# Attention between batches in the last encoder: two tiles of four heads a step

## The chip, the cores and the metric

The kernel runs on one NeuronCore of one Trainium2 chip. Its engines are TensorE (PE, with its weight loads PEld), VectorE (DVE), ScalarE (ACT), GpSimd (POOL) and SyncE (SP), each with a queue of its own. The metric is the device time of one execution in microseconds; lower is better.

## The reference

Four layers follow each other on x of 8 batches, 256 tokens and 128 channels. The last one's encoder holds the attention of this case. It attends between batches: its sequence is the batch index, and each of the 256 token places is a problem of its own with 8 queries and 8 keys.

```python
def _mha(x, w, b, ow, ob):          # L = 8 batches, N = 256 places, H = 4 heads, HD = 32
    L, N, _ = x.shape
    qkv = x @ w.T + b
    q, k, v = jnp.split(qkv, 3, axis=-1)
    rh = lambda t: t.reshape(L, N, H, HD).transpose(1, 2, 0, 3)
    q, k, v = (rh(q), rh(k), rh(v))
    scores = jnp.einsum('nhld,nhmd->nhlm', q, k) / np.float32(np.sqrt(HD))
    attn = jax.nn.softmax(scores, axis=-1)
    o = jnp.einsum('nhlm,nhmd->nhld', attn, v).transpose(2, 0, 1, 3).reshape(L, N, D)
    return o @ ow.T + ob
```

Around it stand layer norms and a mixture of eight experts, which the change does not touch.

## The kernel before

The kernel is a chain of stages, each of several programs (nc.Block); all engines meet at the end of a program. encoder3 (L2730) calls batch_attention (L2960) first.

The 2048 tokens are laid in 16 tiles of 128: a tile holds 16 token places of all 8 batches. The scores of a tile are 128x128 per head; a mask table, same_token, is 0 where two columns belong to the same place and -1e30 elsewhere, so that the softmax runs over the 8 batches of one place.

After a layer norm and the transposing of the weights there are three programs:
- Queries, keys and values (L2993 to L3034): PE makes queries and keys by channels (L3000) into the four banks of psS, DVE copies them with bias and in tile order (L3018), ACT permutes x (L3028), PE makes the values by tokens (L3008), and DVE adds their bias (L3022). A bank is overwritten once DVE has copied it.
- Attention (class SmallAttention, L2743): 64 units, each of one tile and one head, written as two loops over the 16 tiles, one loop for two heads. For a unit DVE masks the queries to the rows of one head (L2856), PE makes the scores over all 128 rows (L2827), DVE adds the mask and takes the maximum (L2872) and negates it (L2884), ACT takes the exponential with a running sum (L2919), PE transposes (L2835), DVE and ACT in turn copy the result (L2910), PE multiplies by the head's 32 value columns (L2847), and DVE takes the reciprocal (L2895) and scales the product into att_out (L2897). PE's order interleaves the scores of the next unit with the transpose and the product of this one. Exponentials, copies and transposes are each of one unit.
- Projection (L3057 to L3093): PE transposes the 16 tiles of att_out (L3066), ACT copies them back to token order (L3082), PE multiplies by the output weights (L3071), DVE has added the bias to XN meanwhile (L3088) and adds the product (L3092).

Of the kernel before, what the change touches and what calls it, by code (L numbers as in the profile page):

```python
# [52 lines left out]
def constants():  # L53
# [37 lines left out]
    tables["swap"] = swap  # L91
    place, at = {}, 0
# [2650 lines left out]
class SmallAttention:  # L2743
# [3 lines left out]

    masked_queries = True

    def __init__(self, k, mem, chunks, groups, hd, heads, masks=False, like=None):
        self.k, self.chunks, self.groups, self.hd, self.heads, self.masks = k, chunks, groups, hd, heads, masks
        self.NC, self.G = len(chunks), len(groups)
        width = chunks[-1][0] + chunks[-1][1]
        if like is not None:
            self.q = like.q
            self.prob = like.prob  # L2760
            self.probT = like.probT
            self.masked = like.masked
            self.peak = like.peak
            self.shift = like.shift
            self.sums = like.sums
            self.total = like.total
            self.rtotal = like.rtotal
            self.waiter = like.waiter
        else:
            self.q = k.sb("att_q", [P, 2, P], ctx=mem)  # L2770
            self.prob = k.sb("att_prob", [P, 2, width], ctx=mem)
            self.probT = k.sb("att_probT", [P, self.G, BANK], ctx=mem)
            self.masked = k.sb("att_masked", [P, width], ctx=mem) if masks else None
            self.peak = k.sb("att_peak", [P, 2, self.NC], ctx=mem)
            self.shift = k.sb("att_shift", [P, 2], ctx=mem)
            self.sums = k.sb("att_sums", [P, 2, self.NC], ctx=mem)
            self.total = k.sb("att_total", [P, 2], ctx=mem)
            self.rtotal = k.sb("att_rtotal", [P, 2], ctx=mem)
            self.waiter = k.sb("att_waiter", [P, 2, self.NC], ctx=mem)
        self.q_ready, self.score_ready = k.flag("q_ready"), k.flag("score_ready")  # L2780
        self.peak_done, self.shift_ready = k.flag("peak_done"), k.flag("shift_ready")
        self.exp_done, self.turned = k.flag("exp_done"), k.flag("turned")
        self.values_done, self.total_done = k.flag("values_done"), k.flag("total_done")
        self.rtotal_done, self.out_free = k.flag("rtotal_done"), k.flag("out_free")
        self.slot = [k.psO[:, 0, 0:hd], k.psM[:, 0:hd]]
        self.copied = [k.flag("copied_by_dve"), k.flag("copied_by_act")]

    def finish(self, blocks):

        units = blocks * self.heads * 2  # L2790
        self.q_ready.passed(units if self.masked_queries else 0)
        self.score_ready.passed(units * self.NC)
        self.peak_done.passed(units * self.NC)
        self.shift_ready.passed(units)
        self.exp_done.passed(units * self.NC)
        self.turned.passed(units * self.G)
        self.values_done.passed(units)
        self.total_done.passed(units if self.NC > 1 else 0)
        self.rtotal_done.passed(units)
        self.out_free.passed(units + 2)  # L2800
        self.copied[0].passed(units * self.G // 2 + 1)
        self.copied[1].passed(units * self.G // 2 + 1)

    def credit(self, eng, engine):

        if engine == "dve":
            eng.sem_inc(self.out_free.sem, 2)
            eng.sem_inc(self.copied[0].sem, 1)  # L2810
        else:
            eng.sem_inc(self.copied[1].sem, 1)

    def pe_step(self, pe, keys_of, values_of, score=None, value=None):

        k, nc, NC, G = self.k, self.k.nc, self.NC, self.G
        for c in range(max(NC, G) + 2):
            if value is not None and c < max(NC, G):
                j, s, h = value

                pe.wait_ge(*self.exp_done((j * 2 + s) * NC + c + 1))
            if score is not None and c < NC:
                js, ss, hs = score
                if c == 0:
                    pe.wait_ge(*self.q_ready(js * 2 + ss + 1))
                c0, w = self.chunks[c]
                nc.tensor.matmul(k.psS[:, c, 0:w], self.q[:, ss, :], keys_of(hs, ss, c0, w),  # L2827
                                 start=True, stop=True).then_inc(self.score_ready.sem, 1)
            if value is not None and c < G:
                n = s * G + c  # L2830

                pe.wait_ge(*self.copied[n % 2](j * G + n // 2 + 1))
                at = 0
                for b, (col, w) in enumerate(self.groups[c]):
                    last = nc.tensor.transpose(k.psT[0:w, n % 2, b * P:(b + 1) * P],  # L2835
                                               self.prob[:, s, col:col + w], k.ident)
                last.then_inc(self.turned.sem, 1)
            g = c - 2
            if value is not None and 0 <= g < G:
                n = s * G + g  # L2840
                if g == 0:

                    pe.wait_ge(*self.out_free(j * 2 + s + 1))

                pe.wait_ge(*self.copied[n % 2](j * G + n // 2 + 2))
                for b, (col, w) in enumerate(self.groups[g]):
                    last = nc.tensor.matmul(self.slot[s], self.probT[0:w, g, b * P:(b + 1) * P],  # L2847
                                            values_of(h, s, g, b, w),
                                            start=(g == 0 and b == 0), stop=(g == G - 1 and b == len(self.groups[g]) - 1))
                if g == G - 1:  # L2850
                    last.then_inc(self.values_done.sem, 1)

    def dve_queries(self, dve, q_of, s, h):

        src, head_column = q_of(h, s)
        self.k.nc.vector.tensor_scalar(self.q[:, s, :], src, head_column, None, ALU.mult).then_inc(self.q_ready.sem, 1)  # L2856

    def dve_step(self, dve, out_of, mask_of, score=None, value=None):
        k, nc, NC, G = self.k, self.k.nc, self.NC, self.G
        for c in range(max(NC, G)):  # L2860
            if score is not None and c < NC:
                j, s, h = score
                c0, w = self.chunks[c]
                if not self.masks:
                    dve.wait_ge(*self.score_ready((j * 2 + s) * NC + c + 1))
                    nc.vector.tensor_reduce(self.peak[:, s, c:c + 1], k.psS[:, c, 0:w], AX_X,
                                            ALU.max).then_inc(self.peak_done.sem, 1)
                else:

                    dve.wait_ge(*self.score_ready((j * 2 + s) * NC + c + 1))  # L2870
                    nc.vector.memset(self.waiter[:, s, c:c + 1], 0.0)
                    nc.vector.tensor_tensor_reduce(out=self.masked[:, c0:c0 + w], in0=k.psS[:, c, 0:w],  # L2872
                                                   in1=mask_of(s, c0, w), scale=1.0, scalar=NEG_BIG, op0=ALU.add,
                                                   op1=ALU.max, accum_out=self.peak[:, s, c:c + 1]).then_inc(self.peak_done.sem, 1)
            if value is not None and c < G:
                jv, sv = value[0], value[1]
                n = sv * G + c
                if n % 2 == 0:
                    dve.wait_ge(*self.turned((jv * 2 + sv) * G + c + 1))
                    self.copy(nc.vector.tensor_copy, c, 0, self.copied[0])  # L2880
        if score is not None:

            dve.wait_ge(*self.peak_done((j * 2 + s) * NC + NC))
            nc.vector.tensor_reduce(self.shift[:, s:s + 1], self.peak[:, s, :], AX_X, ALU.max,  # L2884
                                    negate=True).then_inc(self.shift_ready.sem, 1)
        if value is not None and len(value) == 3:
            jv, sv, hv = value

            dve.wait_ge(*self.values_done(jv * 2 + sv + 1))
            total = self.sums[:, sv, 0:1]  # L2890
            if NC > 1:
                total = self.total[:, sv:sv + 1]
# [7 lines left out]
    def copy(self, how, g, bank, signal):  # L2900
# [3 lines left out]
        for b, (col, w) in enumerate(group):  # L2904
            if runs and runs[-1][2] == w:
                runs[-1][1] = b + 1
            else:
                runs.append([b, b + 1, w])
# [405 lines left out]
```

## Time and profile before

| | us |
|---|---|
| median of 3 runs | 5033.36 (5023.75 to 5037.87) |
| profiled execution, first to last instruction | 5038.9 |
| PE busy in it | 4122.8 (82%) |
| DVE busy | 3247.9 (64%) |
| ACT busy | 2417.4 (48%) |
| POOL busy | 1405.9 (28%) |
| mean granted clock of PE | 0.865 |

The span runs from the first to the last instruction of the profiled execution; the page gives no other time of that execution, so its span stands for it. Busy shares are means over stages that have different limits: what counts for this change is the stretch from 4682 to 4870 us. In the rows below, x48 is a count of records, and an fp32 matmul is two records (a transpose is one). "128*64 128x256" is a weight tile of 128 rows and 64 columns and a moving operand of 256 columns. The granted clock has two levels, 1.2 and 2.4 GHz; 0.50 means that the lower one was granted throughout, and a matmul's own duration shows which it ran at.

### The profile page before, as it was taken

The page shows a single profiled execution, that of the slowest core. Times are in us where ns is not written, and L with a number is a line of the kernel's source. Part 1 is how long each engine was busy: PE and PEld are TensorE (multiplying, and loading weights), DVE is VectorE, ACT ScalarE, POOL GpSimd, SP SyncE. Part 2 cuts the span into 40 slices and gives each one's busy share as a digit, 9 for nine tenths or more (in the row PEclk, how much of TensorE's full clock was granted, in tenths as well). Part 3 has the DMA queues.
Part 4 walks back from the last instruction along what each step waited for, and adds up shares of the span by engine and source line. Part 5 has one row for each costly group of instructions (what it writes and reads, how often), then busy time and mean ns, then how long its engine had stood idle before and what let it go on. Part 6 is the DMA issues. An engine that isn't in the chain of part 4 may idle for free. (4 is left out here: it accounts for less than half of the span.)

```text
span 5038.9 us, 78227 instructions
## 1 busy us (share of the span) xinstructions
PE 4122.8 (82%) x28631; PEld 2518.8 (50%) x28631; DVE 3247.9 (64%) x5963; ACT 2417.4 (48%) x4632; POOL 1405.9 (28%) x1137
## 2 busy tenths in 40 slices
PE   3499999589299965688877899999999999998554
PEld 2133333378033323466664566666666666665342
DVE  3499999422377647433333687888787778887546
ACT  2288888233199840233331455555555554554320
POOL 0200000000300000111100466566566566665000
PEclk6599999699599975677778999999999999999557
DMA  5222221000354200000000000000000000000001
GB/s 155 63 53 46 42 54 33 1 24 14 59 82 75 41 3 17 7 0 0 0 7 27 26 14 1 14 1 14 1 14 14 1 14 1 1 1 1 5 9 38
DMA packets 119688, 122.83 MB, mean 24 GB/s; under 512 B 21264, under 2 KB 97648, under 8 KB 118992
## 3 DMA queue, kind: packets, MB, share of 16 engines
q1 hardware_dynamic: 119240, 118.20, 11.0%
q8 instruction: 197, 3.23, 0.3%
q14 instruction: 107, 0.88, 0.1%
q10 hardware_dynamic: 144, 0.52, 0.0%
HBM read 102.94 MB, written 15.73 MB: 24 GB/s over the span
## 5 line engine op out<-in xcount | busy, mean ns | idle before, releaser
L831 DVE TENSOR_REDUCE att_peak.1<-psS 128x1 f32<-128x512 f32 (+1 forms) x1024 | 580.4, 631 | 94.2 <-PE psS L701 94.1
L2633 POOL TENSOR_TENSOR key_sums_0.1<-key_sums_0.1,prob_0.1 128x512 f32<-128x512 f32 x256 | 402.4, 1572 | 29.0 <-POOL key_sums_0.1 L2628 0.4
L800 ACT ACTIVATE att_probT.1<-psT 128x512 f32<-128x512 f32 (+1 forms) x682 | 368.7, 568 | 75.7 <-PE psT L730 34.3
L2633 POOL TENSOR_TENSOR key_sums_1.1<-key_sums_1.1,prob_1.1 128x512 f32<-128x512 f32 x256 | 386.1, 1508 | 28.7 <-POOL key_sums_1.1 L2633 0.4
L831 DVE TENSOR_REDUCE att_peak.2<-psS 128x1 f32<-128x512 f32 (+1 forms) x512 | 266.8, 568 | 145.0 <-PE psS L701 143.2
L2472 ACT COPY prob_0.1<-psS 128x1024 f32<-128x1024 f32 (+1 forms) x224 | 203.7, 954 | 323.3 <-PE psS L2371 323.3
L701 PE MATMUL psS<-key_stack.1,query_stack.1 64*128 64x512 bf16 (+1 forms) x1024 | 271.1, 386 | 94.1 <-DMA key_stack.1<-key_parts 47.3
L2472 ACT COPY prob_1.1<-psS 128x1024 f32<-128x1024 f32 (+1 forms) x224 | 203.7, 954 | 296.3 <-PE psS L2371 296.3
L747 PE MATMUL psM<-att_probT.1,quad_values.1 128*9 128x256 f32 (+1 forms) x3840 | 306.0, 391 | 19.4 <-issue 19.4
L2542 DVE TENSOR_TENSOR att_highest.1<-att_highest.1,prob_1.1 128x1024 f32<-128x1024 f32 (+1 forms) x160 | 280.4, 1753 | 53.7 <-ACT prob_1.1 L2472 46.4
L2542 DVE TENSOR_TENSOR att_highest.1<-att_highest.1,prob_0.1 128x1024 f32<-128x1024 f32 (+1 forms) x160 | 270.8, 1692 | 56.5 <-ACT prob_0.1 L2472 49.9
L1934 POOL TENSOR_TENSOR head_queries.1<-queryT.1,query_sin.1 64x256 f32<-64x256 f32 x128 | 92.2, 720 | 699.3 <-DVE queryT.1 L2002 691.8
L2628 POOL TENSOR_TENSOR key_sums_0.1<-prob_0.1 128x512 f32<-128x512 f32 x64 | 95.8, 1496 | 587.9 <-ACT prob_0.1 L2478 587.9
L701 PEld LDWEIGHTS psS<-key_stack.1,query_stack.1 64*128 64x128 bf16 x1024 | 78.2, 93 | 352.8 <-issue 192.3
L2563 DVE TENSOR_TENSOR prob_0.1<-prob_0.1,psO 128x1024 f32<-128x1024 f32 (+1 forms) x256 | 245.8, 1011 | 0.0
L2563 DVE TENSOR_TENSOR prob_1.1<-prob_1.1,psO 128x1024 f32<-128x1024 f32 (+1 forms) x256 | 245.7, 1010 | 0.0
L803 ACT ACTIVATE att_probT.2<-psT,att_key_bias.1 128x256 f32<-128x256 f32 (+1 forms) x554 | 224.0, 480 | 27.6 <-PE psT L730 23.8
L2351 PE MATMUL psT<-wkv.1,ctxT_0.1 128*128 128x128 f32 (+1 forms) x1664 | 214.3, 280 | 12.9 <-DVE ctxT_1.1 L2521 12.9
L2351 PE MATMUL psT<-wkv.1,ctxT_1.1 128*128 128x128 f32 (+1 forms) x1664 | 214.6, 280 | 10.9 <-DVE ctxT_0.1 L2521 9.7
L701 PE MATMUL psS<-key_stack.2,query_stack.2 102*128 102x512 bf16 (+1 forms) x512 | 144.5, 367 | 94.7 <-DMA key_stack.2<-mask_parts 87.8
L2341 PE MATMUL psM<-ctxT_0.1,wkv.1 128*128 128x512 f32 (+1 forms) x512 | 215.5, 544 | 3.3 <-ACT keyT_0.1 L2455 1.9
L2351 PEld LDWEIGHTS psT<-wkv.1,ctxT_0.1 128*128 128x128 f32 (+1 forms) x1664 | 192.2, 187 | 50.7 <-issue 31.4
(675 smaller groups left out, 9298.7 us busy)
## 6 DMA issues: line engine op xcount, KB each, us to landing
key_stack.1<-key_parts SPq DMA_DIRECT2D x384, 58.0 KB
key_stack.2<-key_parts SPq DMA_DIRECT2D x96, 200.1 KB
ctx_rows.1<-in_ctx_dram SPq DMA_DIRECT2D x8, 1536.0 KB
key_parts<-split_parts.1 SPq DMA_DIRECT2D x8, 1200.8 KB, 5.7
ctx_keys_0.1<-in_ctx_dram SPq DMA_DIRECT2D x4, 768.0 KB
ctx_keys_1.1<-in_ctx_dram SPq DMA_DIRECT2D x4, 768.0 KB
query_stack.1<-query_parts SPq DMA_DIRECT2D x192, 16.0 KB
ctx_values_0.1<-in_ctx_dram SPq DMA_DIRECT2D x4, 768.0 KB
```

The lines of the kernel that those rows point to most:

```text
L701: self.k.nc.tensor.matmul(self.score_bank[m % 3][:, 0:w], self.queries(rows, g, h, s * P, P), self.keys(rows, g, h, c0, w), start=True, st ...
L747: last = self.k.nc.tensor.matmul(self.partial[32 * j:32 * j + self.hd + 1, :], self.vquad[0:w, q % 2, blk, j, :], self.probT[0:w, g % self ...
L800: last = self.k.nc.scalar.activation(probs[:, blks[0]:blks[-1] + 1, :].rearrange("p b q -> p (b q)"), bank[0:w, 0:len(blks) * S], ACT.Exp)
L803: last = self.k.nc.scalar.activation(probs[:, blk, :], bank[0:w, n * S:(n + 1) * S], ACT.Exp, bias=bias)
L831: self.k.nc.vector.tensor_reduce(self.peak[:, 2 * h + s, c:c + 1], self.score_bank[m % 3][:, 0:w], AX_X, ALU.max).then_inc(self.peak_done. ...
L2341: last = nc.tensor.matmul(bank[:, 0:w], self.wkv[:, t, p * P:(p + 1) * P], self.ctxT[b % 2][:, t, n * BANK:n * BANK + w], start=(t == 0), ...
L2351: last = nc.tensor.matmul(bank[0:w, kb % 4 * P:(kb % 4 + 1) * P], self.ctxT[b % 2][:, t, kb * P:kb * P + w], self.wkv[:, t, at:at + P], st ...
L2472: nc.scalar.copy(self.prob[i % 2][:, :, at:at + w], k.psS[:, 2 * (g % 2):2 * (g % 2) + 2, 0:w]).then_inc(self.kept.sem, 1)
L2542: self.k.nc.vector.tensor_tensor(own, old, new, ALU.max).then_inc(self.raised.sem, 1)
L2563: self.k.nc.vector.tensor_tensor(own, own, by, ALU.add).then_inc(self.lowered.sem, 1)
L2628: nc.gpsimd.tensor_tensor(acc, own[:, h, 0:BANK], own[:, h, BANK:2 * BANK], ALU.add).then_inc(self.summed.sem, 1)
L2633: nc.gpsimd.tensor_tensor(acc, acc, own[:, h, c * BANK:(c + 1) * BANK], ALU.add).then_inc(self.summed.sem, 1)
```

## The change

The 64 units become 8, each of two tiles with all four heads, and the loops are written out. The queries are stored twice, scaled, with rows 0-31 and 64-95 in one copy and rows 32-63 and 96-127 in the other, the rest zero, so that a head's scores need only one half of PE's rows (64). The mask goes into the score banks by a bf16 matmul with the identity, ahead of the scores that accumulate on it. DVE takes the maximum of all 8 score blocks in one instruction, ACT runs 8 exponentials, DVE sums, POOL normalises, PE transposes 8 blocks, ACT copies them in one instruction, and PE multiplies by the values with the values as weights: each head writes its own 32 rows of the output, which is thereby already transposed. DVE copies it to XT in token order. The projection follows in the same program; its transposes and ACT copies are gone.

The steps are staggered: in step s PE makes the scores of unit s, turns unit s-2 and multiplies the values of unit s-3; DVE takes the maximum of s, the sum of s-1, and copies s-3 out; ACT takes the exponential of s and copies s-2.

```diff
+    tables["pair_rows"] = (p[:, None] // 32 % 2 == np.arange(2)) * (np.float32(1) / np.sqrt(np.float32(32)))
...
-class SmallAttention:
...
-        xp, qp, kp = k.sb("x_tiles", [P, N], ctx=mem), k.sb("query_tiles", [P, N], ctx=mem), k.sb("key_tiles", [P, N], ctx=mem)
+        xp, kp = k.sb("x_tiles", [P, N], ctx=mem), k.sb("key_tiles", [P, N], ctx=mem)
+        qp = [k.sb(f"query_tiles_{a}", [P, N], ctx=mem) for a in range(2)]
...
+                for c in range(4):
+                    dve.wait_ge(*qkv_done(c + 1))
+                    for a in range(2):
+                        last = nc.vector.tensor_scalar(permuted(qp[a], c), k.psS[:, c, :].rearrange("p (l i n) -> p l i n", l=2, n=PL),
+                                                       bias[:, 0:1], pair_rows[:, a:a + 1], ALU.add, ALU.mult)
+                    last.then_inc(qkv_copied.sem, 1)
...
+            @block.gpsimd
+            def _(pool):
+                nc.gpsimd.tensor_copy(same[:], k.table("same_token").unsqueeze(1).broadcast_to([P, 4, P])).then_inc(masks_made.sem, 1)
+                nc.gpsimd.tensor_copy(ident[:], k.ident).then_inc(masks_made.sem, 1)
...
-        att = SmallAttention(k, mem, [(0, P)], [[(0, P)]], hd, TILES, masks=True)
...
+        def place(tile, h):
+            return h // 2 * 4 + tile * 2 + h % 2
...
+                def make_scores(u):
+                    if u >= 2:
+                        pe.wait_ge(*exp_done(u - 1))
+                    z = u % 2
+                    for a in range(2):
+                        nc.tensor.matmul(k.psS[:, 2 * z + a, :], ident[:], same[:].rearrange("p j n -> p (j n)"), start=True, stop=False)
+                    for tile in range(2):
+                        cols = slice((2 * u + tile) * P, (2 * u + tile + 1) * P)
+                        for h in (0, 2, 1, 3):
+                            half = slice(h // 2 * 64, h // 2 * 64 + 64)
+                            last = nc.tensor.matmul(unit_scores[z][:, place(tile, h), :], qp[h % 2][half, cols], kp[half, cols], start=False, stop=(tile == 1 and h % 2 == 1))
+                    last.then_inc(score_ready.sem, 1)
+
+                def turn(u):
+                    pe.wait_ge(*normalised(u + 1))
+                    if u >= 1:
+                        pe.wait_ge(*copied(u))
+                    for tile in range(2):
+                        for h in range(H):
+                            last = nc.tensor.transpose(turned_bank[:, tile * 4 + h, :], prob[:, u % 3, place(tile, h), :], k.ident)
+                    last.then_inc(turned.sem, 1)
+
+                def multiply_values(u):
+                    pe.wait_ge(*copied(u + 1))
+                    if u >= 2:
+                        pe.wait_ge(*unit_done(u - 1))
+                    for tile in range(2):
+                        for h in range(H):
+                            own = slice(h * hd, (h + 1) * hd)
+                            last = nc.tensor.matmul(unit_out[u % 2][own, tile * P:(tile + 1) * P], val[:, 2 * u + tile, own],
+                                                    probT[:, u % 2, tile * 4 + h, :], start=True, stop=True)
+                    last.then_inc(values_done.sem, 1)
+
+                for s in range(UNITS + 3):
+                    if s < UNITS:
+                        make_scores(s)
+                    if 0 <= s - 2 < UNITS:
+                        turn(s - 2)
+                    if 0 <= s - 3 < UNITS:
+                        multiply_values(s - 3)
+                pe.wait_ge(*unit_done(UNITS))
...
+                for s in range(UNITS + 2):
+                    if s < UNITS:
+                        act.wait_ge(*shift_ready(s + 1))
+                        if s >= 3:
+                            act.wait_ge(*turned(s - 2))
+                        for j in range(8):
+                            last = nc.scalar.activation(prob[:, s % 3, j, :], unit_scores[s % 2][:, j, :], ACT.Exp, bias=shift[:, s % 2, j:j + 1])
+                        last.then_inc(exp_done.sem, 1)
+                    if 0 <= s - 2 < UNITS:
+                        u = s - 2
+                        act.wait_ge(*turned(u + 1))
+                        if u >= 2:
+                            act.wait_ge(*values_done(u - 1))
+                        nc.scalar.copy(probT[:, u % 2].rearrange("p j n -> p (j n)"),
+                                       turned_bank.rearrange("p j n -> p (j n)")).then_inc(copied.sem, 1)
+
+            @block.gpsimd
+            def _(pool):
+                for u in range(UNITS):
+                    pool.wait_ge(*rtotal_done(u + 1))
+                    x = prob[:, u % 3]
+                    nc.gpsimd.tensor_tensor(x, x, total[:, u % 2, :].unsqueeze(2).broadcast_to([P, 8, P]), ALU.mult).then_inc(normalised.sem, 1)
...
+                for s in range(UNITS + 3):
+                    if s < UNITS:
+                        dve.wait_ge(*score_ready(s + 1))
+                        if s >= 2:
+                            dve.wait_ge(*exp_done(s - 1))
+                        nc.vector.tensor_reduce(shift[:, s % 2, :], unit_scores[s % 2], AX_X, ALU.max, negate=True).then_inc(shift_ready.sem, 1)
+                    if 0 <= s - 1 < UNITS:
+                        u = s - 1
+                        dve.wait_ge(*exp_done(u + 1))
+                        if u >= 2:
+                            dve.wait_ge(*normalised(u - 1))
+                        nc.vector.tensor_reduce(total[:, u % 2, :], prob[:, u % 3], AX_X, ALU.add).then_inc(summed.sem, 1)
+                        dve.wait_ge(*summed(u + 1))
+                        nc.vector.reciprocal(total[:, u % 2, :], total[:, u % 2, :]).then_inc(rtotal_done.sem, 1)
+                    if 0 <= s - 3 < UNITS:
+                        u = s - 3
+                        dve.wait_ge(*values_done(u + 1))
+                        nc.vector.tensor_copy(by_tile[:, 2 * u:2 * u + 2], unit_out[u % 2].rearrange("p (i l n) -> p i l n", i=2, n=PL)).then_inc(unit_done.sem, 1)
```

The lines of the projection that stay (L3070 to L3073, L3087 to L3093) follow these loops unchanged, DVE's bias addition ahead of its loop.

## Rows read from the trace of the kernel before

**Rows 1.** Busy time by stretch, the two loops of the attention program (columns: stretch, length, PE, PEld, DVE, ACT, POOL, clock).
```profile
4696.20:4784.30 88.10, 50.93 (x160) 34.87 (x160) 36.59 (x238) 40.57 (x96) 0.00 (x0) 0.52 0.00 0
4784.30:4859.20 74.90, 52.48 (x162) 35.62 (x161) 36.26 (x242) 20.04 (x80) 0.00 (x0) 0.50 0.00 0
```
**Rows 2.** Waits in the attention program: total us, times, longest.
```profile
ACT att_prob.2 L2919 <- DVE att_shift.5 L2884: 59.2, 33, 2.8
ACT att_probT.4 L2910 <- PE psT L2835: 40.2, 32, 1.3
```
**Rows 3.** Groups of instructions in the attention program: mask and maximum.
```profile
L2872 DVE CUSTOM_DVE_ANT_0 att_masked.1<-psS,tables.1 128x128 f32<-128x128 f32 x64 | 18.3, 286 | 20.3 <-issue 17.1
```
**Rows 4.** Instructions of L2919 (ns min/median/max, first and last start), and a hand-off in the timeline.
```profile
L2919 ACT ACT_TABLE_LOAD  x16: 1283/1283/1283, 4696.3 to 4779.2; - x16
...
4740.07 0.27 ACT L2910 COPY att_probT.4<-psT 128x128 f32<-128x128 f32 x1 [1.29 <-PE psT L2835]
...
4740.62 0.63 PE L2847 MATMUL psM<-values.2,att_probT.4 128*128 x2 [0.58 <-ACT att_probT.4 L2910]
```
**Rows 5.** Timeline, the program of the output projection.
```profile
4859.32 2.29 DVE L3088 TENSOR_TENSOR XN.1<-XN.1,out_bias.1 128x2048 f32<-128x2048 f32 x1 [0.33 <-PEq L3039]
...
4860.44 3.33 ACT L3082 COPY XT.1<-psS 128x128 f32<-128x128 f32 x16 [2.69 <-PE psS L3066]
...
4863.83 5.50 PE L3071 MATMUL psS<-in_projT.1,XT.1 128*128 128x128 f32 x32 [0.86 <-ACT XT.1 L3082]
```
**Rows 6.** Timeline, the program of queries, keys and values.
```profile
4684.39 0.75 DVE L3018 TENSOR_SCALAR query_tiles.1<-psS,in_proj_bias.1 128x512 f32<-128x512 f32 x1 [2.05 <-PE psS L3000]
...
4686.10 0.75 DVE L3018 TENSOR_SCALAR query_tiles.1<-psS,in_proj_bias.1 128x512 f32<-128x512 f32 x1 [0.96 <-PE psS L3000]
...
4688.93 3.33 DVE L3018 TENSOR_SCALAR key_tiles.1<-psS,in_proj_bias.1 128x512 f32<-128x512 f32 x4
...
4691.31 3.73 PE L3008 MATMUL psS<-in_projT.1,x_tiles.1 128*128 128x128 f32 x32
...
4695.08 0.69 DVE L3022 TENSOR_TENSOR values.2<-psS,value_bias.1 128x512 f32<-128x512 f32 x1 [0.20 <-PE psS L3008]
```
**Rows 7.** Timeline of PE in earlier stages: small matmuls, row halves, transposes.
```profile
2300.22 0.27 PE L1852 MATMUL psS<-causal_bf16.1,ident_bf16.3 128*128 128x256 bf16 x1
...
2300.33 0.60 PE L1851 MATMUL psS<-keyT.1,head_queries.1 128*128 128x256 f32 x2
...
2301.31 0.97 PEld L1876 LDWEIGHTS psO<-values.1,att_probT.3 128*128 128x128 f32 x8
...
2608.99 0.60 PE L2037 MATMUL psS<-tables.1,att_out.3 128*128 128x128 f32 x4
2609.43 1.06 PE L2029 MATMUL psO<-wo.1,att_outT.2 128*128 128x128 f32 x8
...
3999.63 1.68 PE L2371 MATMUL psS<-qT_0.1,keyT_0.1 64*128 64x256 f32 x14
```
**Rows 8.** Timeline of PE in the second stage: column quarters, then row halves.
```profile
522.73 0.62 PE L747 MATMUL psM<-att_probT.1,quad_values.1 128*9 128x256 f32 x8
523.28 0.39 PE L701 MATMUL psS<-key_stack.1,query_stack.1 64*128 64x512 bf16 x2
```
**Rows 9.** POOL's additions: in the timeline with DVE idle, and in groups.
```profile
4636.06 5.39 POOL L2633 TENSOR_TENSOR key_sums_1.1<-key_sums_1.1,prob_1.1 128x512 f32<-128x512 f32 x4
...
L2633 POOL TENSOR_TENSOR key_sums_0.1<-key_sums_0.1,prob_0.1 128x512 f32<-128x512 f32 x256 | 402.4, 1572 | 29.0 <-POOL key_sums_0.1 L2628 0.4 <-POOL key_sums_0.1 L2633 0.4
L2637 POOL TENSOR_TENSOR key_sums_1.1<-key_sums_1.1,prob_1.1 66x256 f32<-66x256 f32 x64 | 85.1, 1329 | 9.2
```
**Rows 10.** Groups of instructions by form: DVE's maximum, ACT's exponential and copy.
```profile
L1974 DVE TENSOR_REDUCE att_shift.3<-psS 128x4 f32<-128x1024 f32 x32 | 39.2, 1224 | 48.9 <-PE psS L1852 48.9
...
L1943 ACT ACTIVATE att_prob.1<-psS,att_shift.3 128x128 f32<-128x128 f32 x128 | 45.2, 366 | 47.7 <-DVE att_shift.3 L1974 47.7
...
L2472 ACT COPY prob_0.1<-psS 128x1024 f32<-128x1024 f32 x192 | 185.0, 1015 | 258.6 <-PE psS L2371 258.6
```

More of the change, by code:

```diff
@@ L2740, in encoder3 @@
         scale_and_shift(k, k.XN, affine["ln2_g"], affine["ln2_b"], add_to=k.X)
-class SmallAttention:
[L2752 to L2892, printed above, removed]
-                nc.vector.tensor_reduce(total, self.sums[:, sv, :], AX_X, ALU.add).then_inc(self.total_done.sem, 1)
-                dve.wait_ge(*self.total_done(jv * 2 + sv + 1))
-            nc.vector.reciprocal(self.rtotal[:, sv:sv + 1], total).then_inc(self.rtotal_done.sem, 1)
-            dve.wait_ge(*self.rtotal_done(jv * 2 + sv + 1))
-            nc.vector.tensor_scalar(out_of(hv, sv), self.slot[sv], self.rtotal[:, sv:sv + 1], None,
-                                    ALU.mult).then_inc(self.out_free.sem, 1)
-    def copy(self, how, g, bank, signal):
-        k, group = self.k, self.groups[g]
-        runs = []
[L2904 to L2908, printed above, removed]
-        for b0, b1, w in runs:
-            last = how(self.probT[0:w, g, b0 * P:b1 * P], k.psT[0:w, bank, b0 * P:b1 * P])
-        last.then_inc(signal.sem, 1)
-    def act_unit(self, act, j, s):
-        k, nc, NC, G = self.k, self.k.nc, self.NC, self.G
-        for c, (c0, w) in enumerate(self.chunks):
-            if c == 0:
-                act.wait_ge(*self.shift_ready(j * 2 + s + 1))
-            src = k.psS[:, c, 0:w] if not self.masks else self.masked[:, c0:c0 + w]
-            nc.scalar.activation(self.prob[:, s, c0:c0 + w], src, ACT.Exp, bias=self.shift[:, s:s + 1],
-                                 accum_out=self.sums[:, s, c:c + 1]).then_inc(self.exp_done.sem, 1)
-        for g in range(G):
-            if (s * G + g) % 2 == 1:
-                act.wait_ge(*self.turned((j * 2 + s) * G + g + 1))
-                self.copy(nc.scalar.copy, g, 1, self.copied[1])
-    def pe_run(self, pe, j0, keys_of, values_of):
-        H = self.heads
-        self.pe_step(pe, keys_of, values_of, score=(j0, 0, 0))
-        if H > 1:
-            with pe.Fori(0, H - 1) as h:
-                self.pe_step(pe, keys_of, values_of, score=(j0 + h, 1, h), value=(j0 + h, 0, h))
-                self.pe_step(pe, keys_of, values_of, score=(j0 + h + 1, 0, h + 1), value=(j0 + h, 1, h))
-        last = j0 + (H - 1)
-        self.pe_step(pe, keys_of, values_of, score=(last, 1, H - 1), value=(last, 0, H - 1))
-        self.pe_step(pe, keys_of, values_of, value=(last, 1, H - 1))
-    def dve_run(self, dve, j0, q_of, out_of, mask_of=None):
-        H = self.heads
-        self.dve_queries(dve, q_of, 0, 0)
-        self.dve_queries(dve, q_of, 1, 0)
-        self.dve_step(dve, out_of, mask_of, score=(j0, 0, 0))
-        if H > 1:
-            with dve.Fori(0, H - 1) as h:
-                self.dve_queries(dve, q_of, 0, h + 1)
-                self.dve_step(dve, out_of, mask_of, score=(j0 + h, 1, h), value=(j0 + h, 0, h))
-                self.dve_queries(dve, q_of, 1, h + 1)
-                self.dve_step(dve, out_of, mask_of, score=(j0 + h + 1, 0, h + 1), value=(j0 + h, 1, h))
-        last = j0 + (H - 1)
-        self.dve_step(dve, out_of, mask_of, score=(last, 1, H - 1), value=(last, 0, H - 1))
-        self.dve_step(dve, out_of, mask_of, value=(last, 1, H - 1))
-    def act_run(self, act, j0):
-        with act.Fori(0, self.heads) as h:
-            for s in range(2):
-                self.act_unit(act, j0 + h, s)
@@ L3034, in batch_attention @@
         v_copied.passed(4)
[L3036 to L3038 removed]
+        masks_made.passed(2)
+        unit_scores = [k.psS[:, 2 * z:2 * z + 2, :].rearrange("p a (j n) -> p (a j) n", n=P) for z in range(2)]
+        unit_out = [k.psO[:].rearrange("p a n -> p (a n)")[:, 0:2 * P], k.psM[:, 0:2 * P]]
+        turned_bank = k.psT[:].rearrange("p a (j n) -> p (a j) n", n=P)
+        by_tile = k.XT[:].rearrange("p (l i n) -> p i l n", l=B, n=PL)
+        def place(tile, h):
+            return h // 2 * 4 + tile * 2 + h % 2
         with nc.Block() as block:
@@ L3059, in batch_attention @@
-        att.finish(H // 2)
-        with nc.Block() as block:
-            @block.tensor
-            def _(pe):
-                for t in range(TILES):
-                    last = nc.tensor.transpose(k.psS[:, t // 4, (t % 4) * P:(t % 4 + 1) * P], out[:, t, :], k.ident)
-                    if t % 4 == 3:
-                        last.then_inc(turned.sem, 1)
-                pe.wait_ge(*copied(4))
+                def make_scores(u):
[10 more added lines that the diff above has]
+                    last.then_inc(score_ready.sem, 1)
```

51 lines of the change are left out of this document (20 added, 31 removed).

## The prediction

> **What bounds the kernel now.** I read the busy time by stretch first. The attention program of the last encoder takes 88.1 us for its first two heads and 74.9 us for the other two, and in neither is an engine full: PE is busy 51 and 52 us, DVE 37 and 36, ACT 41 and 20, POOL 0, at a granted clock of 0.52 and 0.50 [rows 1]. A stage in which nobody is full is bound by hand-offs, and the table of waits says by which: ACT waits 59 us for DVE's shift and 40 us for PE's transpose, each time for the step just before its own [rows 2]. Each unit (one tile, one head, 64 in all) runs score, mask and maximum, exponential, transpose, copy, value product, scaling through four engines, on operands of 128 columns or less. The groups show how small they are: mask and maximum of a unit take 0.29 us [rows 3]. The instructions of one line and the timeline give the cadence. In the first program loop a table load of 1.28 us stands ahead of every second unit, 16 of them from 4696.3 to 4779.2, so a round of two units takes 82.9/15 = 5.53 us; the second loop has none and takes 74.9/16 = 4.68 us a round [rows 1, 4]. Behind it stand 16 transposes with 16 small copies of ACT that end at 4863.8, and then the projection, 5.5 us of matmuls [rows 5].
>
> Nothing runs beside this program, so what it loses the end of the kernel loses.
>
> **Removed.** From 4696.3 (the program's first table load [rows 4]) to 4863.83 (first projection matmul [rows 5]) is 167.5 us; all of it is replaced. The projection and its four additions stay.
>
> **Added ahead of it, in the program of queries, keys and values.** Each query bank is now copied twice. DVE's copies come 0.83 us apart when they are not waiting (3.33 us for four [rows 6]), and two are needed in place of one while PE delivers a bank every 1.71 us at first (4684.39 to 4686.10). DVE ends the query copies at 4684.39 + 8 x 0.82 = 4690.9, the keys at 4694.2, the values, 0.72 us apart, at 4697.1, where before the last value copy ended at 4695.77 [rows 6]. That is +1.35 us: only the values' waits for PE covered it before. The two bf16 copies on POOL have 10 us of idle POOL beside them and cost nothing; without that cover they would cost some 1.5 us, by POOL's 1.35 us for 512 columns [rows 9]. The second scalar operand (multiply behind add) I price at zero, at most 8 x 0.08 us.
>
> **The new loop, per unit of two tiles and four heads.** PE, at full clock:
> - Mask: two bf16 matmuls of 512 columns. A 256-column bf16 pass starts 0.11 us ahead of the next matmul (2300.22 to 2300.33) [rows 7], so 2 x 0.22 = 0.44 us.
> - Scores: 8 fp32 matmuls, 16 records, over 64 rows and 128 columns. The full-height 128x128 ones take 3.73/16 = 0.233 us each [rows 6]. The nearest row-half pairs are those of L2371: 14 records of 256 columns in 1.68 us, 0.12 a record, where one after the other they would be 0.21 (two passes of 256 columns at 2.4 GHz); so halves do overlap there. But 0.12 is also what a record costs that is all weight load, 8 of them in 0.97 us for matmuls of 32 columns [rows 7]. With 128 columns to stream, the weight loads bound: 16 x 0.115 = 1.8 us (0.115 is half of the 0.233 of a full-height matmul). Low end, loads overlapping too: 0.9 us.
> - Eight transposes: 4 from 2608.99 to 2609.43, 0.44 us [rows 7], so 0.9 us.
> - Values by quarters: 4 fp32 matmuls of 256 columns, 8 records, go in 0.55 us (522.73 to 523.28), against 1.7 one after the other [rows 8]. With 128 columns I take 0.35 us, twice: 0.7 us. High end: 8 x 0.22 = 1.8 us.
> - Four changes of the array's shape, 0.07 us each: 0.3 us.
>
> In all 4.1 us (3.0 to 5.2); at half clock, where a pass takes twice as long, about 7.6 (the changes of shape not doubled, the values overlapping as before).
>
> DVE: maximum over 1024 columns 1.22 us [rows 10], sum 1.22, reciprocal 0.25 with its wait, copy of 256 columns 0.43: 3.1 us. ACT: 8 exponentials without accumulator; they have 0.27 us each if they follow like the 128-column copies (0.21 apart, [rows 5]) plus the exponential's longer pass, at most 0.366 each [rows 10]: 2.15 us (to 2.9), and a copy of 1024 columns 1.02 us [rows 10]: 3.2 us. POOL: normalising 1024 columns, two inputs: 512 take 5.39/4 = 1.35 us when DVE leaves it alone and 1.57 in the mean of the run [rows 9], so 2.65 (to 3.1) us.
>
> So no engine alone needs more than 4.1 us. But PE's own order ties them: turn(s-2), values(s-3), scores(s+1), then DVE's max(s+1) and sum(s), then POOL, then turn(s), which is two units on. Two units cost 4.1 + 1.22 + 1.47 + 2.65 + four hand-offs of 0.1 = 9.8 us: **4.9 us a unit**, PE busy five sixths of it. This is the new wait: PE stands at turn() for POOL, and behind it on PE's queue stand the values of the unit before and the next scores, for which DVE and ACT wait.
>
> The loop: the first turn at 2.6 (scores; DVE's bias addition of 2.29 us [rows 5] and ACT's one table load, 1.28 us, lie beside them) + 1.3 + 2.2 + 1.6 + 2.7 = 10.4 us. The eighth turn is 7 units later, 34.3 us, less 2.8 us because the last two rounds have no scores: 31.5. Then turn, copy, values and last copy 1.0 + 1.1 + 0.9 + 0.6 = 3.6. That is 45.5 us; PE starts 0.27 us late behind ACT and 0.1 behind DVE at each of its some 16 waits (in the old loop a copy ends at 4740.34 and PE's matmul is at 4740.62 [rows 4]), of which I count 2.5 us: **48 us**. Then the projection as before, 6.2 us; at full clock it would be 1.8 us less, which I leave in the range.
>
> **Sum.** 167.5 - 48 - 1.35 = 118.2 us gained. The profiled execution spans 5038.9 us, 5.5 us (0.1%) above the median of the three runs shown, 5033.4; against its span 4920.7, against the median **4915**. Runs of this kernel differ by 14 us (0.3%); 0.3% is what a measurement can tell from no change.
>
> **A rule weighed.** Where value quarters meet row-half scores, the group of 8 records takes 0.55 us from start to start, of which 256 x 4 columns at 2.4 GHz are 0.43: 0.12 us is left for the change of shape and the first weights [rows 8]. The Trainium skill (TensorEngine Tiling (Array Packing), Key Properties) says that changing the tiling mode, not just the tile, drains TensorE; it gives no figure. By the rows a drain costs at most that remainder: 32 changes of 0.12 us are 3.8 us in the loop where the sum has 2.2, and the time would be 4917.
>
> **Rivals.**
> 1. *Half clock holds through the loop* (chance 0.17). For it: the old loop ran at 0.50 with PE busy 70% [rows 1]. Against: the program ahead ends at full speed (0.233 a matmul), and at half clock PE would have no idle time. PE then bounds at 7.6 us a unit: 10.4 + 51 + 4 = 65 us, gain 101, time 4932.
> 2. *The quarters don't run side by side* (0.06), so part of the change doesn't do what it says: +1.1 us a unit on the pair's chain at full clock, loop 52, time 4919; with half clock, 9.8 us a unit, loop 81, time 4948.
> 3. *Row halves load weights side by side as well* (0.12): PE 3.0 us a unit, the pair 8.7, loop 43, time 4910.
> 4. *POOL is the bound* (0.04): a broadcast factor along 128 columns has no row. At the worst row, 66x256 in 1.33 us beside DVE [rows 9], 1024 columns take 5.3 us; the pair is 12.5, loop 60, time 4927.
> 5. *Slower than before* (0.01): the same normalisation falls to an element-wise slow path. It decides once a unit takes over 20.7 us (166/8), that is a POOL multiply of some 20 us, 7.5 times its nearest row. Nothing in the trace is like that.
>
> **Numbers.** Forecast 0.60: 4905 to 4922. The range takes rivals 1, 3, 4, the lighter half of 2, and 7 us of scatter on either side: 4900 to 4945. Every case but the last ends more than 15 us below the median: faster 0.97; 0.02 for no difference I can see now (a stall that takes the whole gain), slower 0.01.
>
> **What would show it.** In the changed profile: about 48 us between the program's start and the first projection matmul; PE idle before transposes, released by POOL's product, in every unit; 16 score records in about 1.8 us; value groups of 16 records in 0.7; POOL's product near 2.65 us; one table load; the value copies ending 1.3 us later. Wrong it is if PE waits nowhere and runs at half clock (rival 1), if POOL's product is over 4 us, or if ACT's exponentials are over 0.4 us apart, since then ACT at 4.2 us is level with PE.

## The result, and the profile after

The changed kernel takes 4900.1 us (median of 4, 4898.2 to 4905.1) against 5028.6 us (median of 4, 5023.8 to 5037.9) for the kernel before: 0.9739 of its time, 95% interval 0.9725 to 0.9754. That is 128.5 us less, where the prediction had 118.2. The profiled executions span 4903.2 and 5038.9 us, 135.7 us apart. By stretches, between the starts of the same layer norms and programs:

| stretch | before | after | difference |
|---|---|---|---|
| all ahead of the last encoder's layer norm | 4669.4 | 4662.8 | -6.5 (unchanged code) |
| layer norm to attention program | 26.9 | 27.7 | +0.8 |
| attention program (from its first table load) to first projection matmul | 167.5 | 38.2 | -129.3 |
| projection to next layer norm | 6.6 | 5.1 | -1.5 |
| the rest | 168.5 | 169.3 | +0.8 |

The 6.5 us lie in stages that no edit touches. Such a difference says nothing: in two profiled executions of the changed kernel the attention program starts at 4690.5 and at 4677.5 us, 13 us apart. So the change itself is worth some 129 us. The busy time by stretch, of the kernel after, for the attention program and the projection (columns as in rows 1):

```profile
4690.50:4728.80 38.30, 25.91 (x333) 18.64 (x337) 25.81 (x33) 25.97 (x73) 15.16 (x8) 1.00 0.00 1
4728.80:4733.60 4.80, 3.80 (x32) 3.61 (x32) 2.77 (x4) 0.00 (x0) 0.00 (x0) 1.00 0.01 3
```

Against [rows 1] DVE issues 33 instructions for 480, ACT 73 for 176, and POOL 8 for none. PE issues no fewer: 333 records for 322. Yet it is busy 25.9 us for 103.4, because it is at its full clock, 1.00 for 0.50, and because the row halves of its array work side by side (shown below), as by their times the column quarters do too. The timeline of the kernel after shows one unit and the waits in it (weight loads left out):

```profile
4702.73 1.09 PE L2878 MATMUL psT<-tables.1,att_prob.2 128*128 128x128 f32 x8 [0.27 <-POOL att_prob.2 L2929]
...
4703.75 0.64 PE L2888 MATMUL psO<-att_probT.4,values.2 128*32 128x128 f32 x16
...
4704.33 0.60 PE L2864 MATMUL psS<-same_token_bf16.1,ident_bf16.4 128*128 128x512 bf16 x2
...
4704.86 0.49 PE L2869 MATMUL psS<-key_tiles.1,query_tiles_0.1 64*128 64x128 f32 x4
...
4705.64 0.39 PE L2869 MATMUL psS<-key_tiles.1,query_tiles_1.1 64*128 64x128 f32 x4
...
4706.07 1.23 DVE L2940 TENSOR_REDUCE att_shift.5<-psS 128x8 f32<-128x1024 f32 x1 [0.69 <-PE psS L2869]
...
4707.22 1.21 DVE L2946 TENSOR_REDUCE att_total.1<-att_prob.2 128x8 f32<-128x1024 f32 x1
4707.33 2.17 ACT L2914 ACTIVATE att_prob.2<-psS,att_shift.5 128x128 f32<-128x128 f32 x8 [0.50 <-DVE att_shift.5 L2940]
...
4708.74 1.90 POOL L2929 TENSOR_TENSOR att_prob.2<-att_prob.2,att_total.1 128x1024 f32<-128x1024 f32 x1 [1.68 <-DVE att_total.1 L2948]
...
4710.69 1.09 PE L2878 MATMUL psT<-tables.1,att_prob.2 128*128 128x128 f32 x8 [0.28 <-POOL att_prob.2 L2929]
```

Read it as the chain of the prediction. Turn and values take 1.60 us (4702.73 to 4704.33), mask and scores 1.74 (to 4706.07), the maximum 1.15 until the sum starts, sum and reciprocal 1.52 until POOL starts, POOL 1.95 until PE turns again: 7.96 us for two units. Between them PE turned once more, at 4707.12. The 16 score records go in 1.0 us (4704.86 to about 4705.9), less than their four groups' busy times added. In a later kernel (ACT's copy first, below) where the next turn follows them without a wait, it starts 1.09 us behind them (4697.03 to 4698.12).

### The profile page after: what moved, and what is told of

Read it like the earlier page. It is cut to its first block and busy times, and to the rows that moved or that the text cites. A ratio compares the mean times of both kernels' runs of the same rounds, so it can differ in the third digit from the quotient of the medians.

```text
span 4903.2 us, 76709 instructions
## 1 busy us (share of the span) xinstructions
PE 4032.0 (82%) x28627; PEld 2455.7 (50%) x28631; DVE 3202.5 (65%) x5519; ACT 2379.5 (49%) x4513; POOL 1422.2 (29%) x1147
## 5 line engine op out<-in xcount | busy, mean ns | idle before, releaser
L832 DVE TENSOR_REDUCE att_peak.2<-psS 128x1 f32<-128x512 f32 (+1 forms) x512 | 266.7, 569 | 137.6 <-PE psS L702 135.7
```

What stands on the lines that cost most here:

```text
L832: self.k.nc.vector.tensor_reduce(self.peak[:, 2 * h + s, c:c + 1], self.score_bank[m % 3][:, 0:w], AX_X, ALU.max).then_inc(self.peak_done. ...
```

## The experiments

The measures are the length of the attention program (from the start of its first table load to the first projection matmul) and, for the steady part, the time from one turn of PE to the next but one ("the pair"): 38.2 and 7.96 us in the changed kernel. Experiments that alter the changed kernel come first, then two that alter the kernel before. Each was executed once, except where rounds are named. The same changed kernel had a program of 38.2 us in one execution and of 41.3 in another, with the same pair (last section), so the pair is the firmer measure. A single whole time can't show such differences: the kernel with POOL's product twice has a program 16 us longer and took 4902.2 us.

**Row halves one after the other.**

```diff
-                    for tile in range(2):
-                        cols = slice((2 * u + tile) * P, (2 * u + tile + 1) * P)
-                        for h in (0, 2, 1, 3):
+                    for top in (0, 2):
+                        for tile, h in ((0, top), (0, top + 1), (1, top), (1, top + 1)):
+                            cols = slice((2 * u + tile) * P, (2 * u + tile + 1) * P)
```

> The eight scores of a unit are issued with the four of one row half behind each other, then the four of the other. Theory one (the two-unit chain turn, values, scores, maximum, sum, POOL, turn sets the pace; 3.98 us a unit in the changed kernel): a group of 16 score records goes from about 0.98 to 1.8 us, the chain holds one group in two units, so the pair goes from 7.96 to about 8.8 us and the attention program (first table load to first projection matmul) from 38.2 to about 42 us. Theory two (row halves never overlapped, weight loads bound, as the forecast priced them): no change.

The pair goes to 8.50 us and the program to 43.7. In the timeline of this kernel a group of mask and scores runs from 4709.31 to about 4711.5:

```profile
4709.31 0.60 PE L2864 MATMUL psS<-same_token_bf16.1,ident_bf16.4 128*128 128x512 bf16 x2
4709.84 0.48 PE L2869 MATMUL psS<-key_tiles.1,query_tiles_0.1 64*128 64x128 f32 x2
4710.17 0.38 PE L2869 MATMUL psS<-key_tiles.1,query_tiles_1.1 64*128 64x128 f32 x2
...
4711.17 0.38 PE L2869 MATMUL psS<-key_tiles.1,query_tiles_1.1 64*128 64x128 f32 x2
```

The scores alone take 1.5 us for 1.0. Within one half a matmul of two records starts every 0.22 us (4710.95 to 4711.17), much as at full height (0.233, [rows 6]); alternating, a group of four records does (4705.41 to 4705.64). So the halves do overlap, their weight loads with them: in the changed kernel one load of the scores lasts 0.19 us in the mean of the records, and 16 of them start within the 1.0 us. Half a microsecond more in the group is half a microsecond more in the pair: theory one, with a smaller size than expected (the change of half inside a group still overlaps once). The program's further 3.6 us are of another kind: three of the eight turns took 1.97 us for 1.09, the low clock (see the last section).

**POOL with a full second operand, and POOL twice.**

```diff
-                    nc.gpsimd.tensor_tensor(x, x, total[:, u % 2, :].unsqueeze(2).broadcast_to([P, 8, P]), ALU.mult).then_inc(normalised.sem, 1)
+                    nc.gpsimd.tensor_tensor(x, x, kp[:, 0:8 * P].rearrange("p (j n) -> p j n", n=P), ALU.mult).then_inc(normalised.sem, 1)
```

> POOL multiplies by a full 128x1024 tensor in place of a factor repeated along 128 columns (the normalisation is left out). If POOL's 1.90 us came from the repeated operand, the product takes 2.6 to 2.7 us, the rate of the additions in the trace of before, the pair of units goes from 7.96 to 8.7 us and the program from 38.2 to about 41.2 us. If the operand does not matter, 1.9 us and no change anywhere.

```profile
4701.03 2.35 POOL L2929 TENSOR_TENSOR att_prob.2<-att_prob.2,key_tiles.1 128x1024 f32<-128x1024 f32 x1 [3.55 <-DVE att_total.1 L2948]
```

2.35 us for 1.90, and the pair 8.42 for 7.96: the 0.45 us of the product come back as 0.46 in the pair. The program takes 41.9 us, 3.7 more: 1.6 by the pairs, the rest with a turn of 1.57 and one of 1.97 us, at the low clock in part or whole. The repeated operand makes POOL cheaper, but by little more than half of what I had expected: two additions of 512 columns took 2.7 us [rows 9], so 0.35 us is left. POOL's fixed part, which counts once, is part of that: with one tile a unit (below) a product of 512 columns takes 1.04 us, and two of those are 0.18 over the 1.90. The other 0.17 isn't shown; those rows are additions, and no run multiplied and added at the same length.

```diff
+                    nc.gpsimd.tensor_tensor(x, x, total[:, u % 2, :].unsqueeze(2).broadcast_to([P, 8, P]), ALU.mult).then_inc(pool_half.sem, 1)
+                    pool.wait_ge(*pool_half(u + 1))
```

> POOL multiplies twice (the result is scaled twice, which changes its values). Theory one (chain through POOL): 2 us more in each pair, 7.96 to about 9.9 us, and the program from 38.2 to 46 or 47 us. Theory two (an engine's own work sets the pace, PE or ACT with 3.2 to 3.4 us a unit): POOL's 3.9 us a unit are still under the 3.98 us of now, so the program stays within 2.5 us (the last unit's own extra product) of 38.2.

The program takes 54.5 us, the pair 12.6 at first and 11.5 in the later part. POOL is not the bound (four products of 1.90 us are 7.6 in a pair of 11.5), so theory two falls; but the later pair rose by 3.55 us, not by 2. The missing part stands in PE's rows:

```profile
4704.97 1.87 PE L2879 MATMUL psT<-tables.1,att_prob.2 128*128 128x128 f32 x8 [3.41 <-POOL att_prob.2 L2932]
4706.77 1.08 PE L2889 MATMUL psM<-att_probT.4,values.2 128*32 128x128 f32 x16
...
4707.78 0.96 PE L2865 MATMUL psS<-same_token_bf16.1,ident_bf16.4 128*128 128x512 bf16 x2
```

PE had stood 3.41 us for POOL, and the turn, the values and most of the mask then ran at the low clock: 1.80, 1.01 and 0.89 us where they take 1.0, 0.58 and 0.53, so 1.6 us. The second product adds 1.97 us until POOL is done (4703.02 less 4701.05), and the two together are the 3.5 us. In the pair of 12.6 us the scores ran at the low clock as well (2.0 us for 1.09).

**Turning one unit later.** A fourth buffer of probabilities; every s - 2 and s - 3 of the loops becomes s - 3 and s - 4.

```diff
-                    if 0 <= s - 2 < UNITS:
-                        turn(s - 2)
-                    if 0 <= s - 3 < UNITS:
-                        multiply_values(s - 3)
+                    if 0 <= s - 3 < UNITS:
+                        turn(s - 3)
+                    if 0 <= s - 4 < UNITS:
+                        multiply_values(s - 4)
```

> A fourth buffer of probabilities; PE turns unit s-3 and multiplies the values of s-4, ACT copies s-3. Theory one: PE no longer stands for POOL in the steady part, a unit falls from 3.98 to about 3.4 us (PE's or ACT's own work), the program from 38.2 to 35 or 36 us, since one more step of filling gives back about 1 us. Theory two (throughput is already the bound): 3.98 us a unit stay, and the program gets longer by the extra step.

A miss for theory one by its numbers (3.4 us a unit, a program of 35 or 36): the pair is 7.80 us and the program 39.9. But PE no longer stands for POOL; it stands for ACT:

```profile
4709.15 2.18 ACT L2914 ACTIVATE att_prob.2<-psS,att_shift.5 128x128 f32<-128x128 f32 x8 [1.74 <-DVE att_shift.5 L2940]
...
4711.17 1.06 ACT L2921 COPY att_probT.4<-psT 128x1024 f32<-128x1024 f32 x1
...
4712.38 1.06 PE L2878 MATMUL psT<-tables.1,att_prob.2 128*128 128x128 f32 x8 [1.30 <-ACT att_probT.4 L2921]
```

There is one turned bank, so a turn needs ACT's copy of the unit before, and that copy stands in ACT's queue behind exponentials which need the scores that PE made after its last turn: scores, maximum, exponentials, copy, turn, 7.8 us here, only 0.16 under the 7.96 of POOL's chain in the changed kernel. A new theory follows, a second chain of almost the same length, and this kernel with ACT's copy moved ahead of its exponentials tests it:

> As the kernel that turns one unit later, but ACT copies unit s-3 out of the turned bank ahead of the exponentials of unit s. In that kernel the pair of units took 7.8 us and PE stood at the turn for ACT's copy, not for POOL. Theory one (a second chain of nearly the same length, scores, maximum, exponentials, copy, turn, took over): with the copy out of it a unit falls to PE's and ACT's own 3.3 to 3.5 us, the pair to 6.9, and the program to 35 to 37 us. Theory two (some engine is already full at 3.9 us): no gain, 39 to 40 us.

The steady pair falls to 6.5 us (6.9 expected) and the program to 34.2:

```profile
4691.50:4701.40 9.90, 9.85 (x130) 7.00 (x127) 8.86 (x13) 9.81 (x31) 6.18 (x4) 1.00 0.01 2
```

PE is busy 9.85 of 9.90 us and ACT 9.81: with both chains cut, the program is at its engines' own pace, 3.23 us a unit. In five rounds against the kernel before:

> The kernel with the turn one unit later and ACT's copy first, timed against the kernel before beside the changed kernel. Its attention program took 34.2 us where the changed kernel's took 38.2, so it should be 4 us (0.08%) under the changed kernel, near 4895 us; that is less than the scatter of single runs, and only the medians can show it, if anything does.

It takes 4894.2 us (4884.3 to 4899.0), ratio 0.9724 (0.9710 to 0.9737), and its program again 34.3 us.

> The changed kernel as it is, in the same rounds: 128 to 131 us under the kernel before, a ratio of 0.974, and an attention program of 38.2 us again, if its course does not depend on the execution.

The changed kernel takes 4900.5 us (4894.5 to 4902.9), ratio 0.9744 (0.9730 to 0.9757). The medians are 6.3 us apart in the expected direction; the intervals overlap, so of the whole time this is an indication, and the programs' lengths are the evidence. This execution of the changed kernel had a program of 41.3 us.

**DVE's sum first.** The two blocks of DVE's loop change places, work and waits the same.

```diff
                 for s in range(UNITS + 3):
+                    if 0 <= s - 1 < UNITS:
+                        ...
                     if s < UNITS:
                         ...
-                    if 0 <= s - 1 < UNITS:
-                        ...
```

> DVE takes the sum of unit s-1 ahead of the maximum of unit s. Theory one: the work is the same but a cycle of exponentials, sum, reciprocal, maximum and again exponentials closes within one unit: 2.17 + 1.21 + 0.25 + 1.22 + hand-offs of 0.2 = 5.1 us a unit, the program from 38.2 to about 46 us. Theory two (throughput of an engine): no change.

The program takes 47.5 us, a unit 4.8:

```profile
4726.72 2.18 ACT L2914 ACTIVATE att_prob.2<-psS,att_shift.5 128x128 f32<-128x128 f32 x8 [1.72 <-DVE att_shift.5 L2948]
...
4728.93 1.22 DVE L2941 TENSOR_REDUCE att_total.1<-att_prob.2 128x8 f32<-128x1024 f32 x1 [1.66 <-ACT att_prob.2 L2914]
...
4731.52 2.18 ACT L2914 ACTIVATE att_prob.2<-psS,att_shift.5 128x128 f32<-128x128 f32 x8 [1.72 <-DVE att_shift.5 L2948]
```

ACT and DVE now wait for each other in turn. The order in one queue is worth 0.8 us a unit here (a unit of 5.1 us was expected, 1.1 more than before). Of the program's 9.3 us, five steady steps are 4.1; 4.2 lie between the first turn and the second (7.1 us for 2.9), where PE ran in part at the low clock, and 1.0 behind the seventh turn, the last one being low (1.95 us).

**One tile a unit.** UNITS = TILES, and four score blocks to an instruction in place of eight.

> Sixteen units of one tile and four heads with instructions of half the size. If the gain came from large instructions (fixed costs paid once for two tiles), a unit of one tile costs well over half of 3.98 us: maximum 0.69, sum 0.69, POOL 1.0, reciprocal 0.25, hand-offs 0.4, PE 1.8: 4.8 us a pair, 2.4 us a unit, 38 us for sixteen and 3 us less filling, so the program stays within 3 us of 38.2. If hand-offs weigh more than that, as in the old loop, it is over 45 us.

The pair is 4.70 us, as worked out, and the program 43.5, 5.3 over the changed kernel and 2.3 over what I allowed: fifteen steps of 2.35 us are 35.0 us from first to last turn, where seven of the larger ones are 25.5. Twice the tiles to a step saves 15% of the steady part (4.70 to 3.98 us for two tiles); it is not what took the old 167 us to 38.

**Quarters one after the other.** The loops over tiles and heads of the values change places.

> The two tiles of one column quarter follow each other, so that at most two quarters can be at work together. If the quarters' overlap carries the 0.58 us of a value group, the group takes about 1.0 us, the pair of units 0.4 us more and the program about 40 us. If the matmuls of one quarter stream behind each other without loss, nothing changes.

A value group takes 0.60 us (4703.72 to 4704.32) for 0.58, the pair 7.98, the program 38.4: no change. Whether the quarters are at work together isn't settled by this, since each may still overlap with the next; that eight matmuls of two records take 0.6 us shows only that they are not one after the other at the 0.233 us of a full-height matmul [rows 6].

**The old attention without its table loads, and written out.**

```diff
                 att.credit(act, "act")
+                nc.scalar.activation(known[:], k.ident[:, 0:1], ACT.Exp)
```

> The kernel before with one exponential of one column ahead of its loops, so that the table set is known on entering them. If the 16 table loads of the first loop are what makes its rounds 5.53 us and not 4.68, one load is left and the kernel gains 13 to 14 us, a tenth of what the change gained. If the loads lie beside other work, it gains nothing.

```diff
-            with pe.Fori(0, H - 1) as h:
+            for h in range(H - 1):
-            with dve.Fori(0, H - 1) as h:
+            for h in range(H - 1):
-        with act.Fori(0, self.heads) as h:
+        for h in range(self.heads):
```

> The kernel before with the three program loops of its attention written out, all else as it was; the table is then loaded once. Theory one (the small instructions' hand-offs made the 167.5 us): the loads bring 13 us as known, register work at most a few us more, so the old attention keeps 140 to 155 us. Theory two (the loops' register and branch work between instructions was a large part, as the idle time put down to issue hints, 31 us ahead of the score weights alone): under 125 us, and that much of the change's gain is only the writing out.

The first takes 153.3 us from its table load to the projection, 14.2 less than the kernel before: the loads were in nobody's shadow. The second, which has a single table load too, takes 133.2 us, another 20.1 less. The waits of the second:

```profile
ACT att_prob.2 L2919 <- DVE att_shift.5 L2884: 47.5, 31, 2.8
ACT att_probT.4 L2910 <- PE psT L2835: 32.4, 30, 1.1
...
PEld psO L2847 <- DVE att_out.4 L2897: 24.6, 29, 0.8
```

It lies between the two theories. The waits for instruction issue, before 31.1 us ahead of PE's weight loads for the scores and 28.6 and 27.3 ahead of those for the values, are gone. Of the 31.1 the table loads had been the larger part (14.1 are left in the kernel without them), and behind the other two stood hand-offs that are still there, 24.6 and 24.5 us for DVE's scaling. So of the 129 us, by one execution each, 14 were table loads and 20 the loops' own work. The other 95 no run splits, but for the two extra passes over the output, 4.5 us (4859.32 to 4863.83, [rows 5]): they are the small steps, the mean clock of 0.51 and the matmuls that now go side by side, together.

## Why the prediction was right or wrong

- **The place and kind of the gain: right, with one chain missing.** The attention program shrank and nothing else moved; PE's new wait is at the turn, for POOL, and the pair's chain is the one that was written down. The experiments on scores and POOL moved the pair by what they moved in the chain; DVE's order closed another cycle within one unit, 4.8 us where 5.1 were worked out. What the prediction did not have is the second chain, through ACT's copy, only 0.16 us shorter; it cost the forecast nothing, but whoever cuts only the predicted chain gains next to nothing.
- **The size of the loop: 48 us forecast, 38.2 measured; the terms of the sum that failed.** The pair had 9.8 us and measured 7.96. POOL's product had 2.65 and took 1.90, priced by additions of half the length with two full operands. PE's part had 4.1 and took 3.34: the scores had 1.8 us, by the reading that weight loads bound row halves as they bound full matmuls, and took 1.0. That is rival 3, which had 0.12 of the chance; 0.60 stood on the other. The reading came from a row in which 0.12 us a record fits both causes, moving columns and weight loads. The remaining 0.3 us is the maximum, which leaves 1.15 to the sum, and the hand-offs. Along the program: the first turn came at 9.3 us for 10.4, first to last turn took 25.5 for 31.5, and the rest 3.4 for 3.6. The 2.5 us for late starts of PE were not there; the delays between engines are inside the 7.96 us of the pair, where the sum had its hand-offs too, so they were counted twice. Together that is the 9.8 us.
- **The range: 4900 to 4945.** The measured 4900.1 lies on its lower edge, and below the 4905 of the narrower forecast. It is 15 us under 4915, of which 4.8 are no error of the sum: the median of the kernel before, 5033.4 then, is 5028.6 with the fourth run. In the gain the sum is 10.3 us short, 128.5 for 118.2. By the profile it is 11.0 us, 129.2 for 118.2: 9.8 in the loop, 0.5 ahead of it (+0.8 for +1.35), and 1.5 in the projection, which ran at full clock and stood only in the range, less 0.8 in the rest. The range's low end was rival 3's 4910 less 7 us of scatter, which is 4903 and was put down as 4900; and rival 3 took 1.1 us off PE where its shorter scores alone are 0.9. Rival 3 together with a cheaper POOL, which is what happened, was not worked out. Both errors had the same sign.
- **The query copies: +1.35 forecast, +0.4 measured** for their program. They came 0.72 us apart and not 0.82. My spacing, taken from copies that were themselves waiting, was too long. The second scalar costs at most 0.04 us a copy: the keys' copies, with one scalar, came 0.68 apart (four in 2.72 us).
- **Rivals 1, 2, 4 and 5** did not come: the clock was 1.00, the values took 0.58 us, POOL's product was short.
- **The rule on drains:** the mask, behind the values, goes from 4704.33 to 4704.86, 0.53 us for 2 x 512 columns that need 0.43 at 2.4 GHz. The remainder of 0.1 us is all that the change of shape behind the mask can cost. The Trainium skill's sentence (TensorEngine Tiling (Array Packing), Key Properties) gives no size for its drain; the trace neither shows one by itself nor leaves room for more there.

## What to carry to other kernels

Where no engine is full, write down the closed chains through the queues (which instruction waits for which, and what stands behind it) and add each one up: here two of 7.96 and 7.80 us set the pace of a program whose engines needed 3.2 a unit, and cutting only the first gained 0.16 us a pair. When a term is taken from the nearest row, ask which resources that row could be bound by; if two fit, carry both into the sum, together with the other terms' bounds of the same sign. A program loop can have costs that its instructions don't show: here a table load on every round of one of two loops, and 20 us of work between the instructions of the loops.

## What the runs showed that I had not expected

- **The same program, 38.2 and 41.3 us.** In the second execution of the changed kernel PE first stood 2.50 us for ACT. The clock fell within the scores that follow (the last four records took 0.63 us for 0.39), so ahead of the wait of 1.53 us for POOL, and the first turn ran low throughout:

```profile
4684.64 0.63 PE L2869 MATMUL psS<-key_tiles.1,query_tiles_1.1 64*128 64x128 f32 x4
...
4686.80 1.97 PE L2878 MATMUL psT<-tables.1,att_prob.2 128*128 128x128 f32 x8 [1.53 <-POOL att_prob.2 L2929]
4688.56 1.06 PE L2864 MATMUL psS<-same_token_bf16.1,ident_bf16.4 128*128 128x512 bf16 x2
...
4712.21 1.97 PE L2878 MATMUL psT<-tables.1,att_prob.2 128*128 128x128 f32 x8 [3.07 <-POOL att_prob.2 L2929]
```

  The seventh turn was low again, behind 3.07 us of waiting. In the first execution PE stood as long for ACT and 2.72 us ahead of its seventh turn, and neither was followed by a low clock. So a wait in a chain costs its own length and then, in some executions, the slower clock behind it; what decides in which isn't shown. The pair was the same in both, and the whole time of the second, 4894.5 us, was even the shortest of its five. The kernel with both chains cut ran its turns at 1.06 to 1.09 us in both of its executions, though a mask and some scores ahead of the first turn were slow in it too.
- **Weight loads of two row halves go together:** 16 score records in 1.0 us, against 1.5 where four matmuls of one half follow each other, and 1.9 for eight full-height matmuls at 0.233 us.
- **POOL and a repeated factor:** 1024 columns in 1.90 us and 512 in 1.04; 1024 take 2.35 with a full second operand.
